# Two-layer graph kernel: another order of transfers on the sync queue in stages B and C

## The reference, cut to what matters

```python
h  = relu(layernorm(x))
x1 = x + (sum over edges into a node of h[src]) / degree @ Wl.T + h @ Wr.T        # 25,000 edges
h  = relu(layernorm(x1))
agg = segment_sum(edge_attr, src)                                                  # 25,000 edges
t  = batchnorm(silu([h, agg] @ W1 + b1));  t = batchnorm(silu(t @ W2 + b2))
out = x1 + t @ W3 + b3
```

## Time and profile before

| what | value |
|---|---|
| median of three runs | 1394.46 us (1392.79 to 1399.84) |
| the profiled execution's own time | 1390.34 us |
| its span, first to last instruction | 1388.5 us |
| around the span | 1.84 us |
| DVE busy | 1084.9 us, 78% |
| PE busy | 1041.1 us, 75% |
| POOL busy | 874.4 us, 63% |
| ACT busy | 857.2 us, 62% |
| HBM read and written | 163.49 and 150.84 MB, 226 GB/s over the span |

### The profile page before, as it was taken

The page is one execution under the profiler, slowest core; times in us unless marked ns, Lnnn a source line. Parts: engine busy times, 40 slices in busy tenths (PEclk is TensorE's granted clock), DMA queues, the critical chain, the costliest instruction groups (busy, mean ns, idle before and its releaser), DMA issues.

```text
span 1388.5 us, 23109 instructions
## 1 busy us (share of the span) xinstructions
PE 1041.1 (75%) x5614; PEld 751.3 (54%) x5614; DVE 1084.9 (78%) x4687; ACT 857.2 (62%) x1688; POOL 874.4 (63%) x625
## 2 busy tenths in 40 slices
PE   0326677677766666675999999999878889998775
PEld 0225555555544444453666666666546765447765
DVE  2446888888887667675999999999937877788966
ACT  1325677677675655662888887878754546669610
POOL 7778887788888888876878787777760000002443
PEclk9969999999999999987999999999989999999999
DMA  9968987877775666658999999999969984216999
GB/s 363 398 248 198 233 214 201 216 172 155 172 164 133 150 148 138 142 126 205 226 250 250 237 260 254 222 259 233 239 165 322 344 300 151 91 61 252 407 408 381
DMA packets 195453, 315.40 MB, mean 227 GB/s; under 512 B 22704, under 2 KB 74326, under 8 KB 192288
## 3 DMA queue, kind: packets, MB, share of 16 engines
q1 hardware_dynamic: 127720, 266.61, 55.5%
q0 software_dynamic: 62720, 38.57, 23.0%
q10 hardware_dynamic: 4920, 9.22, 1.8%
HBM read 163.49 MB, written 150.84 MB: 226 GB/s over the span
## 4 chain that ended last, share of the span: by engine, by line
POOL 42%; DMA 23%; issue 18%; PE 12%; DVE 4%; SPq 1%; ACT 0%; POOLq 0%; DVEq 0%; ACTq 0%
POOL acc L948 21%; POOL acc L969 10%; POOL xin L926 7%; DMA acc<-tabs,target_b 6%; DMA acc<-zT,target_b 6%; PE ps L1793 6%; POOL zT L934 4%; DMA zT<-x_dram 4%; DMA xin<-acc 2%; PE ps L1757 2%; PE ps L1760 1%; DVE zT L1606 1%; DMA acc<-zT,tabs 1%; PE ps L1763 1%; DMA res<-acc 1%
## 5 line engine op out<-in xcount | busy, mean ns | idle before, releaser
L1654 PE MATMUL ps<-zT 128*128 128x512 f32 (+5 forms) x784 | 262.0, 482 | 146.9 <-ACT zT L1089 131.9
L948 POOL DMA_INDIRECT acc<-zT,tabs x196 | 313.1, 1598 | 70.3 <-issue 62.9
L1654 PEld LDWEIGHTS ps<-zT 128*128 128x128 f32 (+1 forms) x784 | 158.6, 209 | 273.8 <-issue 122.3
L1406 DVE BATCH_NORM_STATS2 zT<-zT 128x6 f32<-128x128 f32 (+1 forms) x384 | 78.9, 278 | 168.5 <-DMA zT<-in_x_dram 168.5
L969 POOL DMA_INDIRECT acc<-zT,target_b x100 | 156.3, 1563 | 45.0 <-issue 26.6
L969 POOL DMA_INDIRECT acc<-tabs,target_b x96 | 150.6, 1569 | 42.2 <-issue 24.9
L926 POOL DMA_INDIRECT xin<-in_x_dram,tabs x140 | 141.5, 1011 | 42.7 <-issue 42.4
L1687 PE MATMUL ps<-wlr,hT 128*128 128x128 f32 (+1 forms) x784 | 103.8, 289 | 34.6 <-DVE zT L1397 34.4
L1687 PEld LDWEIGHTS ps<-wlr,hT 128*128 128x128 f32 (+1 forms) x784 | 100.0, 203 | 41.8 <-issue 39.0
L1532 DVE BATCH_NORM_STATS2 stats_place<-zT (+1 forms) x168 | 107.2, 681 | 18.5 <-ACT zT L1192 17.4
L1048 ACT ACTIVATE hT<-ps 128x1024 f32<-128x1024 f32 (+1 forms) x100 | 100.0, 1002 | 32.1 <-PE ps L1646 30.3
(11 more groups left out here) (202 smaller groups left out, 2343.5 us busy)
## 6 DMA issues: line engine op xcount, KB each, us to landing
acc<-zT SPq DMA_DIRECT2D x12, 2112.0 KB, 20.0
acc<-stats_place SPq DMA_DIRECT2D x48, 528.0 KB
zT<-acc SPq DMA_DIRECT2D x97, 256.0 KB
zT<-in_x_dram SPq DMA_DIRECT2D x48, 512.0 KB, 6.6
zT<-x_dram SPq DMA_DIRECT2D x42, 512.0 KB, 9.9
out_dram<-zT SPq DMA_DIRECT2D x42, 512.0 KB, 10.4
zT<-row_dram SPq DMA_DIRECT2D x49, 256.0 KB, 5.7
x_dram<-xin SPq DMA_DIRECT2D x49, 256.0 KB
```

The source lines that it names most:

```text
L948: pool.indirect_dma_start(acc1, bass.IndirectOffsetOnAxis(ap=target_a[:, k, j:j + 1], axis=0), v[:, j, :], None, compute_op=ALU.add).then_ ...
L1654: ins = nc.tensor.matmul(psA[:, 0:j + 1, 0:p], t[0:p, j, :], same[0:p, par, at:at + j + 1, 0:p], start=(j == ROWS - 1), stop=(j == 0))
```

## The change

In `step_b` the landings release other work: chunk 0 the first half of the nodes and the names, chunk 1 the edges and the first half of y, chunk 2 the second halves of nodes and y, chunk 3 both halves of x1. The tail's step waits for x1 alone and stores it. The waits for all x1 stores ahead of C become one wait per place, each ahead of the load that overwrites it. In C the ten fetches stand later between the same reloads: fetches 0 to 2 ahead of the reloads of n = 10, 12 and 14, fetch 3 behind the stores of n = 11 and ahead of reload 15, fetches 4 to 9 one behind each of the reloads 15 to 20. Before, they stood ahead of the reloads 5, 7, 9, 11, 12, 13, 15, 17, 18 and 19. The last z load (`pre_activations(IT)`) and the tail's `acc2` stand behind fetch 9 instead of ahead of fetch 8. Loops of reloads are written out.

```diff
-                for n, scattered in enumerate((after_a(this(s_first2, par, i, 16)), this(s_sc2, par, i, 16))):
-                    sp.wait_ge(*scattered)
-                    if third:
-                        load_b_nodes(n, *third)
-                    if third and third[3]:
...
-                        load_b_y(n, *third)
-                    if n == 0 and 2 * (i + 2) + par <= RF:
-                        load_b_names(i + 2, par)
+                if tail:
+                    sp.wait_ge(*this(B["added"], par, i))
+                    for n in range(2):
+                        store_half(x1_ring[slot], x1_v, 2 * node[0] + node[1], n, tail, x1_stored[slot])
+                    return
+                more_edges = 2 * (i + 2) + par <= RF
+                y_wanted = third and third[3]
+                sp.wait_ge(*after_a(this(s_first2, par, i, 16)))
+                if third:
+                    load_b_nodes(0, *third)
+                if more_edges:
+                    load_b_names(i + 2, par)
+                sp.wait_ge(*this(s_sc2, par, i, 16))
+                if more_edges:
+                    load_b_edges(i + 2, par, i + 2 == IT, 0)
+                if y_wanted:
...
+                    load_b_y(0, *third)
                 sp.wait_ge(*this(s_mid2, par, i, 16))
+                if third:
+                    load_b_nodes(1, *third)
+                if y_wanted:
+                    load_b_y(1, *third)
+                sp.wait_ge(*this(s_end2, par, i, 16))
                 sp.wait_ge(*this(B["added"], par, i))
-                store_half(x1_ring[slot], x1_v, 2 * node[0] + node[1], 0, tail, x1_stored[slot])
-                sp.wait_ge(*this(s_end2, par, i, 16))
-                store_half(x1_ring[slot], x1_v, 2 * node[0] + node[1], 1, tail, x1_stored[slot])
-                if 2 * (i + 2) + par <= RF:
-                    load_b_edges(i + 2, par, i + 2 == IT, 0)
+                for n in range(2):
+                    store_half(x1_ring[slot], x1_v, 2 * node[0] + node[1], n, tail, x1_stored[slot])
...
-            for k in range(RING):
-                r = RF - (RF - k) % RING
-                sp.wait_ge(x1_stored[k], x1_count(r // 2, k, r == RF))
...
-            for n in range(2):
+            for n, first_slot in ((0, 2), (1, 0)):
                 for par in range(2):
+                    k = first_slot + par
+                    r = RF - (RF - k) % RING
+                    sp.wait_ge(x1_stored[k], x1_count(r // 2, k, r == RF))
                     load_c(n, n, n, par)
...
-            reload_fixed(3, 5)
-            fetch(0)
-            reload_loop(5, 7, 1)
+            reload_fixed(3, 7)
             for par in range(2):
                 store_z(C, zz_dram, 3, KEPT_LATER, par)
-            fetch(1)
-            reload_loop(7, 9, 1)
+            reload_fixed(7, 9)
...
+            reload_fixed(9, 10)
+            fetch(0)
+            reload_fixed(10, 12)
+            fetch(1)
+            reload_fixed(12, 14)
             fetch(2)
-            reload_loop(9, MID_C, 1)
+            reload_fixed(14, MID_C + 4)
+            for par in range(2):
+                store_z(C, zz_dram, MID_C, IT - 1, par)
             fetch(3)
-            reload_fixed(MID_C, MID_C + 1)
+            reload_fixed(MID_C + 4, KEPT)
             fetch(4)
...
+            fetch(9)
             sp.wait_ge(C["stored"][1], 32)
             pre_activations(IT, 0, True)
             load_c(IT, IT, 0, 0, True)
-            fetch(8)
-            reload_fixed(KEPT + 2, KEPT + 3)
-            fetch(9)
-            reload_loop(KEPT + 3, IT - 1, 2)
-            reload_fixed(IT - 1, IT)
+            reload_fixed(KEPT + 5, IT)
```

More of the change, by code:

```diff
@@ L711, in step_b @@
                 i, par, tail, spill, slot, node = now
-                for n, scattered in enumerate((after_a(this(s_first2, par, i, 16)), this(s_sc2, par, i, 16))):
-                    sp.wait_ge(*scattered)
-                    if third:
-                        load_b_nodes(n, *third)
-                    if third and third[3]:
-                        if before:
-                            sp.wait_ge(*this(B["act_normed"], *before[1::-1]))
-                        load_b_y(n, *third)
-                    if n == 0 and 2 * (i + 2) + par <= RF:
-                        load_b_names(i + 2, par)
@@ new lines, in step_b @@
+                more_edges = 2 * (i + 2) + par <= RF
[9 more added lines that the diff above has]
+                if y_wanted:
+                    if before:
+                        sp.wait_ge(*this(B["act_normed"], *before[1::-1]))
+                    load_b_y(0, *third)
@@ L772, in reload_fixed @@
                         reload_c(n, iteration_c(n), n % 2, par)
-            def reload_loop(lo, hi, shift):
-                doubled(sp, lambda n, half, odd, par: reload_c(n, n - shift, odd, par), lo, hi)
             def load_late(d, first, i, par, tail, t):
@@ L814, in _ @@
                 pre_activations(IT - 1, par)
-            fetch(2)
-            reload_loop(9, MID_C, 1)
-            fetch(3)
-            reload_fixed(MID_C, MID_C + 1)
[L819 to L822, removed]
+            reload_fixed(9, 10)
[3 more added lines that the diff above has]
+            reload_fixed(12, 14)
+            fetch(2)
+            reload_fixed(14, MID_C + 4)
             for par in range(2):
                 store_z(C, zz_dram, MID_C, IT - 1, par)
+            fetch(3)
+            reload_fixed(MID_C + 4, KEPT)
+            fetch(4)
+            reload_fixed(KEPT, KEPT + 1)
+            fetch(5)
+            reload_fixed(KEPT + 1, KEPT + 2)
             fetch(6)
-            reload_loop(MID_C + 4, KEPT + 1, 2)
+            reload_fixed(KEPT + 2, KEPT + 3)
             fetch(7)
-            reload_fixed(KEPT + 1, KEPT + 2)
+            reload_fixed(KEPT + 3, KEPT + 4)
+            fetch(8)
+            reload_fixed(KEPT + 4, KEPT + 5)
+            fetch(9)
             sp.wait_ge(C["stored"][1], 32)
```

## The result

The changed kernel took **1400.88 us** (median of 20 runs, 1393.54 to 1411.70); the kernel before, run beside it, 1393.62 (20 runs). The ratio is **1.0058, 95% interval 1.0037 to 1.0078**: some 7 us slower, where 4.5 us less were forecast. The profiled execution took 1399.51 us with a span of 1397.6. In the table of experiments the ratio of E13 rests on three of its ten runs, since one run (1376.22 us) lies over 1.5% under most of the others; over all ten its median is 1400.76, beside 1394.33 for the kernel before.

The account below looks back on a forecast made before the run. B was taken as bound by POOL's scatter chain, with DVE next, and C by late transfers on one queue. B 0, tail store 2.1, clock 1.7 and C 0.7 made 4.5 us less: 1390.0 against 1394.46, range 1379 to 1401.

Parts of the forecast that it names:

- order on SP is not what the landings wait for, while a second hardware queue is. I take 0: Stage B's scatters: reordering SP's transfers gains 0, as rounds behind a y step lost least to landings.
- the bound of 8: Stage B: largest loss allowed for the new order, from 256 KB at 241 GB/s in 16 rounds.
- Edges earlier: Late B: edges leave some 3.7 us sooner and close most PE and DVE holes; worth nothing on the path.
- the pre-sum: Stage B: SP's new wait for PE's sum, ahead of y and the second half of the nodes; costs nothing.
- The names and the later y: Stage B: names no longer behind y, and y wanted only three rounds later; both put at nothing.
- The tail's store: Between B and C: the tail's x1 store leaves before the last scatters land, so C's first load leaves 2.1 us sooner.
- PE's clock: Start of C: PE idles 0.45 us, not 2.55, and keeps the upper clock level; 1.7 us gained.
- C's order: Stage C: holes of 5.2 us go and 4.5 come with the later fetches; net 0.7 us gained.
- Six fetches at 0.45: Stage C: fetches 4 to 9, one an iteration, each cost DVE a hole of 0.45 us, 2.7 in sum.
- the tail's loads: End of C: moved behind fetch 9, they cost at n = 21 what they cost at n = 18.
- the slower rival: Stage C: fetches 4 to 9 each wait for the one before and hold reloads; 17 us, total 1404, chance 0.12.
- The hole at n = 7: Stage C: sign that the forecast is right, DVE's hole there under 3 us.

Follow-up runs that it names:

- E13: The changed kernel with C's fetches counted on two semaphores in turn, so fetch k waits for k-2; ratio 0.9973 (0.9916 to 1.0031) to the kernel before.
- E5: The changed kernel with the edges back behind x1's stores, as before the change; ratio 1.0125 (1.0065 to 1.0185) to the kernel before.
- E3: The changed kernel with the halves of y back behind the landings of chunks 0 and 1; ratio 1.0053 (1.0019 to 1.0088) to the kernel before.

## Why the prediction was wrong

**B, "order on SP is not what the landings wait for, while a second hardware queue is. I take 0".** This step failed. It compared kinds of rounds at one order, and there the y step does lose least; but the order decides when in POOL's round ACT's store falls, and that is what costs. The half about the second queue names the right transfer, but took its cost as a constant. The cost is 9.7 us by the means, 9.0 in the profiled pair; the bound of 8 (half of 16 times 1.09 is 8.7) was too low, since it counted 256 KB by bandwidth alone. From the rule of the Trainium skill that it leaned on (DMA: Bandwidth & Descriptors, Queues, rings and completion order: a turn for each queue with work, packet by packet) the forecast read that B gains 0 from any order on one queue; the runs disagree with that reading, with B from 388.6 to 415.3 us for the same transfers. The rule itself need not be false: it tells nothing of when the queues have work.

**Edges earlier, "nothing", and the pre-sum, "nothing".** The edge wait closed nearly as said; what that is worth by itself no run tells. The names and the later y, also put at nothing, came to bind PE and DVE, but only one scatter waited for an engine, 1.3 us. SP's wait for PE's pre-sum was not nothing for SP, 20.0 us, but E5 removed most of it and got slower, so it isn't the loss.

**The tail's store, 2.1 us.** Right: the gap is 6.74 us in seven traces with the old store and 4.42 in eleven with the early one, 2.3 less.

**PE's clock, 1.7 us.** Right in this trace: the first pair takes 0.88 us and not 1.62, the first round 1.93 and not 3.48, and the granted clock stays at the upper of its levels across the gap (1.00 in the idle time and in the first round; before it was 0.95 in the idle time and 0.54 in the first round). The reason given was not right, so this was luck: PE sat idle 3.59 us and not 0.45, longer than the 2.55 after which it was slow before. In E3, with 3.79 idle, the pair takes 1.62. What decides it is open; over the eleven early stores the pair has a mean of 1.14 us, over the seven old ones 1.41, and the first round 2.8 and 3.3, so some half a microsecond is the gain on which to count.

**C's order, 0.7 us gained.** Mis-sized: C loses 4.7 by the means, of which 0.9 lies ahead of DVE's first add and so is not the order's. The first half of the sum was right: up to n = 15 its terms make 1.7 gained (0.35, 1.75 and 1.36 less 1.05 and 0.75), and the means say 1.6, though the forecast overlooked the largest hole of before, the 4.36 at n = 15. The second half failed: from n = 15 to n = 22 its terms make 0.95 lost (2.7 less 1.75), and the means say 5.3, the profiled pair 6.2. Two terms were too small. Six fetches at 0.45 came from fetches that stood apart; here they were issued 4.90 us apart on average (1116.14 to 1140.63, five steps) where an iteration is 3.83. And the tail's loads were to cost at n = 21 what they cost at n = 18, 3.24; behind fetch 9 they left a hole of 5.99. This is the slower rival at no more than a third of its price (4.4 us above the sum, not 14.3), and its point of decision was wrong: it needs no landing of 5.7 us. Five of these landed in 4.21 to 5.56, but as each goes out on the landing of the one before, any landing over one iteration holds SP. The hole at n = 7 is 1.98, under 3, as said; the holes at n = 16 to 21 are not small. By the other figure of the Trainium skill (DMA: Bandwidth & Descriptors, Anatomy of one DMA: an estimated 3.2 us a fetch, by a fit for the GpSimd path) none of this would bind; the trace has 4.2 at least, 5.5 in the median.

**The sum.** By the means +9.7 − 2.3 + 4.7 = 12.1, by times 7.3 (5.2 to 10.9 by the interval). So some 1 to 7 us of these costs do not show at the end. The means are of few traces of single executions, which don't say where. That the range, up to 1401, just holds 1400.88 is luck: the loss is mostly B's, for which the sum had 0. The chance of 0.12 for slower was given to one mechanism, and it came with a second that no rival named.

## What to carry to other kernels

A store on another engine's queue has a phase against the loop that it meets, and an order on one queue shifts that phase: look at when the two meet, round by round, over the whole stage, before an edit is costed at nothing. Where a DMA waits for the landing of the one before on the queue that also carries the loads, it holds that queue each time by what the landing exceeds an iteration; a second semaphore takes that wait away, but not what the loads behind it cost. An average over kinds of rounds at one order tells nothing of another order.

## What the runs showed that was not expected

The same bytes in B, 388.6 to 415.3 us by order alone, and, it seems, a feedback in it: at phases under 4 us a z store costs the next chunk 0 some 1.3 us before and 2.1 changed, at 5.5 and more 0.1 and 0.7, and by the program's order each wait moves the next store towards the costly phase. PE kept the upper granted clock over 3.59 us without a matmul in the changed kernel and had lost it after 2.55 us before.
